# Eight-layer hybrid stack on one Trainium2 core: the index work of the last FFN half in blocks, a two-slot attention lag, and picks dealt by VectorE's load per slot

## What is computed

```python
# FFN 0 (128 -> 512 -> 512 -> 512 -> 128)
h = silu(_tlin(x, w1_w, w1_s)) * _tlin(x, w2_w, w2_s)
h = gelu(_tlin(h, h1_w, h1_s))
h = gelu(_tlin(h, h2_w, h2_s))
return _tlin(h, w3_w, w3_s)
# top-k attention, in batches of 128 queries in the reference's small shape; here one sequence of 2048
I = einsum('bths,h->bts', relu(einsum('bthd,bsd->bths', q_i, k_i)), idx_w)   # 4 index heads
I = where(local, inf, I); I = where(causal, -inf, I)
_, idx = top_k(I, 96)                       # 64 local keys and the 32 best others
key_c, value, kr_sel = rows of the picked keys
scores = (q_c . key_c + q_r . rope(kr_sel, rank)) * scale
out = softmax(scores) . value, then @ W_out
```

## Time and profile before

| | us |
|---|---|
| median of 3 runs (1315.41 to 1323.14) | 1317.44 |
| span of the profiled execution, first to last instruction | 1068.8 |
| PE busy in it | 941.6 |
| DVE busy | 786.1 |
| ACT busy | 692.7 |
| POOL busy | 583.4 |
| mean granted TensorE clock, as a share of 2.4 GHz | 0.893 |

### The profile page before, as it was taken

One profiled execution on the slowest core, in us unless ns is written; L12 is line 12 of the kernel. 1 busy time (PEld: TensorE's weight loads), 2 busy tenths in 40 slices (PEclk: granted clock), 3 DMA queues, 4 the chain that ended last, 5 costly groups with the idle time before them and its releaser, 6 DMA issues. The chain is left out here.

```text
span 1068.8 us, 19776 instructions
## 1 busy us (share of the span) xinstructions
PE 941.6 (88%) x6850; PEld 690.5 (65%) x6850; DVE 786.1 (74%) x1468; ACT 692.7 (65%) x1920; POOL 583.4 (55%) x622
## 2 busy tenths in 40 slices
PE   8999999999999977787889988888988897897786
PEld 5888868676767336556656666666767676576544
DVE  4888875757466788987895898797698979733346
ACT  5767655555564476694695678786687776656454
POOL 0111044333333777777777667777777777776001
PEclk9999999999999678997795689897798978989899
DMA  7100001000000563533522423331331333131001
GB/s 237 40 21 2 2 1 45 1 1 1 1 1 12 124 146 92 132 81 80 130 59 61 101 61 73 73 70 41 73 73 38 73 73 74 47 105 40 1 1 39
DMA packets 58737, 62.07 MB, mean 58 GB/s; under 512 B 27760, under 2 KB 43152, under 8 KB 58256
## 3 DMA queue, kind: packets, MB, share of 16 engines
q1 hardware_dynamic: 42768, 36.41, 13.2%
q0 software_dynamic: 15872, 24.41, 10.1%
HBM read 52.65 MB, written 8.13 MB: 57 GB/s over the span
## 5 line engine op out<-in xcount | busy, mean ns | idle before, releaser
L791 POOL DMA_INDIRECT gathered_rows<-key_table,idx_T x496 | 482.5, 973 | 157.6 <-issue 146.6
L2382 DVE TENSOR_TENSOR turned_rows<-bank,rank_rope 96x512 f32<-96x512 f32 x128 | 87.3, 682 | 83.3 <-PE bank L1293 82.1
L1293 PE MATMUL bank<-ident,gathered_rows 128*96 128x128 f32 x512 | 92.6, 311 | 11.8 <-DVE turned_rows L2382 7.1
L2356 DVE SCALAR_TENSOR_TENSOR index_sums<-index_relu,iw,index_sums 128x512 f32<-128x512 f32 (+4 forms) x114 | 75.4, 661 | 33.4 <-ACT index_relu L1826 30.8
L832 PE MATMUL bank<-index_k_hi,index_q 128*128 128x512 f32 (+5 forms) x160 | 77.2, 485 | 19.3 <-DVE idx_T L2376 11.6
L1826 ACT ACTIVATE index_relu<-bank 128x512 f32<-128x512 f32 (+4 forms) x152 | 75.1, 507 | 24.0 <-PE bank L832 23.6
L1848 ACT ACTIVATE probs<-masked_scores,attn_columns 128x208 f32<-128x208 f32 x128 | 59.5, 465 | 31.3 <-DVE attn_columns L2392 26.7
L832 PE MATMUL bank<-probs_window,local_values 80*32 80x128 f32 x256 | 57.4, 311 | 24.7 <-ACT probs_picked L1864 23.1
L1293 PEld LDWEIGHTS bank<-ident,gathered_rows 128*96 128x96 f32 x512 | 66.0, 144 | 20.5 <-issue 11.4
L2364 DVE MAX8 top<-index_sums 128x8 f32<-128x320 f32 (+13 forms) x56 | 75.8, 1354 | 1.0
L2366 DVE FIND_INDEX8 idx_u<-top,index_sums 128x8 uint32<-128x320 f32 (+13 forms) x56 | 75.5, 1348 | 0.0
(11 more groups left out here) (295 smaller groups left out, 2430.4 us busy)
## 6 DMA issues: line engine op xcount, KB each, us to landing
queries_in<-q_rot SPq DMA_DIRECT2D x32, 256.0 KB
gathered_rows<-key_table,idx_T POOLq DMA_INDIRECT x496, 2.5
q_rot<-rotated SPq DMA_DIRECT2D x16, 256.0 KB, 3.3
queries_in<-q_lat SPq DMA_DIRECT2D x16, 256.0 KB
h<-in_h SPq DMA_DIRECT2D x2, 1024.0 KB, 7.9
q_lat<-q_latent_sb SPq DMA_DIRECT2D x8, 256.0 KB
local_values<-key_table SPq DMA_DIRECT2D x15, 80.0 KB
rope_tables<-in_cos_ql SPq DMA_DIRECT2D x4, 256.0 KB
```

The costliest lines, as they stand in the source:

```text
L791: pool.indirect_dma_start(out=G[i % 2][:, gather_place(i, q), :], out_offset=None, in_=key_table[0:index_width(i), :], in_offset=bass.Indi ...
L1293: last = pe.transpose(bank[2][0:ROW, j * P:(j + 1) * P], G[i % 2][:, gather_place(i, 4 * g + j), :], ident[:])
L2356: v.scalar_tensor_tensor(s_, r_, iw[:, h:h + 1], s_, ALU.mult, ALU.add).then_inc(i_used, 1)
L2382: v.tensor_tensor(GT[n % 2].rearrange("r (j p) -> r j p", j=4), bank[2][0:ROW, :].rearrange("r (j p) -> r j p", j=4), rank_rope[:].unsquee ...
```

## The change

1. POOL no longer rounds the second gelus of R = 3. ACT takes the gelu twice, once into `a_hi` and once into `ffn_full` (`SELF_ROUNDED = 8`); DVE's subtraction waits for ACT. POOL goes from step 7 straight to `gather(0)`; `EARLY_GATHER` is gone.
2. `early_setup` moves everything ahead and into blocks: `raw` and `ik` after q = 0, `iq0` and `iq1` after 1, `iq2` and `iq3` after 2, the sums of tile 0 after 4 with `rows`, `cq` after 5. DVE does the whole pick of tile 0 after its q = 5 and that of tile 1 after its q = 9, with nothing between. PE turns tile 0 after q = 8 and tile 1 after q = 12, and projects `qp0` and `qp1` after 13 and 14, ahead of the downs.
3. The norm of chunks 2 and 3 leaves `topk_front` and is done in the loop (`loop_norm`, slots 7 to 9 and 26 to 28).
4. `ATTN_LAG` goes from 4 to 2, all `TAIL_SLOT` entries down by 2, and the regrouping of the first queries from slots 2 and 3 to slots 0 and 1. SP stores the first rotated queries ahead of the latents.
5. Picks are dealt by room: `other_work(s)` adds up DVE's other elements in a slot, and a slot gets `max(even - other_work(s), even / 4)`.

```diff
-        ATTN_LAG = 4
+        ATTN_LAG = 2
-        TAIL_SLOT = {0: 52, 1: 75, 2: 103, 3: 122}
+        TAIL_SLOT = {0: 50, 1: 73, 2: 101, 3: 120}
+        NORM_SLOT = {2: 7, 3: 26}
+        even = (all_picks + sum(other_work(s) for s in PICKED)) / len(PICKED)
+        room = [max(even - other_work(s), even / 4) for s in PICKED]
...
-                SLOT_STEPS[int(first + (last - first) * run / total) + (step[1] == "rows")].append(step)
+                SLOT_STEPS[slot_with_room(first + (last - first) * run / total) + (step[1] == "rows")].append(step)
...
-                for q in range(4 * NM):
+                for q in range(4 * NM if R < 3 else SELF_ROUNDED):
...
+                    if R == 3 and q >= SELF_ROUNDED:
+                        fn(a_hi[:, q % 8, :], bank[m], ACT.Gelu, scale=sc[:, m:m + 1])
                     fn(f_full[:, q % 4, :], bank[m], ACT.Gelu, scale=sc[:, m:m + 1]).then_inc(f_gelu, 1)
...
-            PICKS_AT = {6: (0, 0, 8), 7: (0, 8, 12), 8: (0, 12, 16), 11: (1, 0, 6), 12: (1, 6, 9), 13: (1, 9, 12), 14: (1, 12, 16)}
+            ENDS_AT = {0: ("ik",), 1: ("iq0", "iq1"), 2: ("iq2", "iq3")}
...
+            def loop_norm(c, k):
+                n = 4 * L_TOPK + c
+                if k == 0:
+                    pe.wait_ge(x_ready, n + 1)
+                    pe.wait_ge(ln_applied, LN0 + n)
+                    bank_released(c - 1, NPIECE - 2)
+                    mm(bank[3], center[:], chunk(x, c)).then_inc(ln_centered, 1)
+                elif k == 1:
+                    pe.wait_ge(ln_squared, n + 1)
+                    bank_released(c - 1, NPIECE - 1)
+                    mm(bank[5], ones[:], chunk(xn, c)).then_inc(ln_var, 1)
```

More of the change, by code:

```diff
@@ L529, in cost, with tail_cost, other_work, slot_with_room @@
             return sum(c for _, c in todo)
+        def tail_cost(g, k):
+            (name, n), W = TAIL[g][k], GROUP_TILES[g][1] * P
+            return {"var": W + 60, "unit": 2 * (HALF + 60), "down": W + 60, "kv": C + 2 * P + 180,
+                    "KV": 2 * P + 60, "lq": C + 60}.get(name, 0)
+        def other_work(s):
+            ends = [PIECES[k] for c, k in piece_ends_at(s)]
+            return (sum(C + 60 for name in ends if name[:2] in ("ik", "iq", "ra", "qp"))
+                    + sum(C + 60 for name in ends if name == "qp0") + 3 * (C + 60) * len(turns_at(s))
+                    + sum(tail_cost(g, k) for g, k in tail_at(s - 1)))
+        PICKED = range(1, PICK_SLOTS)
+        all_picks = cost(sum(SUMS[FRONT + 1:] + PICKS[FRONT:], []))
+        even = (all_picks + sum(other_work(s) for s in PICKED)) / len(PICKED)
+        room = [max(even - other_work(s), even / 4) for s in PICKED]
+        room_before = [sum(room[:k]) * all_picks / sum(room) for k in range(len(room) + 1)]
+        def slot_with_room(work):
+            k = max(k for k in range(len(room)) if room_before[k] <= work + 1e-6)
+            return PICKED[k]
         def spread(todo, first, last):
@@ L1178, in piece @@
                         bank_released(0, PIECES.index(released))
+                elif c == 0 and name[:2] == "qp":
+                    bank_released(0, PIECES.index("rows" if name == "qp0" else "cq"))
                 elif c == 0:
@@ L1215, in early_setup @@
             def early_setup(q):
-                if q == 1:
+                if q == 0:
                     pe.wait_ge(s_tk, N_TK)
                     piece(0, PIECES.index("raw"))
-                elif q == 2:
                     piece(0, PIECES.index("ik"))
-                    piece(0, PIECES.index("iq0"))
-                elif q in (3, 4, 5):
-                    piece(0, PIECES.index(f"iq{q - 2}"))
-                elif q == 6:
+                elif q in (1, 2):
+                    for h in (2 * q - 2, 2 * q - 1):
+                        piece(0, PIECES.index(f"iq{h}"))
+                elif q == 4:
+                    sums(0)
@@ L1226, in early_setup @@
                     piece(0, PIECES.index("rows"))
-                    sums(0)
+                elif q == 5:
+                    piece(0, PIECES.index("cq"))
                 elif q == 7:
-                    piece(0, PIECES.index("cq"))
-                elif q == 9:
                     sums(1)
-                elif q == 10:
+                elif q == 8:
                     index_turn(0)
+                elif q == 12:
+                    index_turn(1)
+                elif q in (13, 14):
+                    piece(0, EARLY + q - 13)
@@ L1249, in topk_front @@
-                norm_var(L_TOPK, 1)
-                for k in range(3, SETUP_FRONT):
-                    piece(1, k)
-                pe.wait_ge(ln_sd, norm_index(L_TOPK, 1) + 2)
+            def loop_norm(c, k):
[9 more added lines that the diff above has]
+                    mm(bank[5], ones[:], chunk(xn, c)).then_inc(ln_var, 1)
@@ L1663, in norm_square, with loop_norm @@
                     fn(chunk(xn, 2 * r + u), bank[4 + u], ACT.Square).then_inc(ln_squared, 1)
+            def loop_norm(c, k):
+                n, own = 4 * L_TOPK + c, chunk(xn, c)
+                if k == 0:
+                    act.wait_ge(ln_centered, n + 1)
+                    fn(own, bank[3], ACT.Square).then_inc(ln_squared, 1)
+                elif k == 1:
+                    act.wait_ge(ln_var, n + 1)
+                    steps.did(fn(own, bank[5], ACT.Ln, scale=1.0 / P, bias=eps_col))
+                    fn(own, own, ACT.Exp, scale=-0.5).then_inc(ln_sd, 1)
             def norm_spread(k, r, which=(0, 1)):
-                if (k, r) != (L_TOPK, 1) and which != (0,):
+                if which != (0,):
                     act.preload_act_table_set("natural_log_exp_and_others")
@@ L2307, in _ @@
             EARLY_PICKS = (SUMS[0] + PICKS[0][:-2], SUMS[1] + PICKS[1][:-2])
-            PICKS_AT = {6: (0, 0, 8), 7: (0, 8, 12), 8: (0, 12, 16), 11: (1, 0, 6), 12: (1, 6, 9), 13: (1, 9, 12), 14: (1, 12, 16)}
+            ENDS_AT = {0: ("ik",), 1: ("iq0", "iq1"), 2: ("iq2", "iq3")}
             def early_setup(q):
-                if 1 <= q < 6:
-                    piece_end(0, q - 1)
-                if q in PICKS_AT:
-                    i, first, last = PICKS_AT[q]
+                for name in ENDS_AT.get(q, ()):
+                    piece_end(0, PIECES.index(name))
+                if q in (5, 9):
+                    i = q // 4 - 1
                     assert len(EARLY_PICKS[i]) == 16
-                    for step, _ in EARLY_PICKS[i][first:last]:
+                    for step, _ in EARLY_PICKS[i]:
                         pick(*step)
-                    if last == 16:
-                        pick(i, "turn", 0)
-                if q == 10:
+                    pick(i, "turn", 0)
+                elif q == 7:
                     pick(0, "rows", 0)
+                elif q == 12:
+                    pick(1, "rows", 0)
             def topk_front():
-                pick(1, "rows", 0)
                 for k in (EARLY, EARLY + 1):
```

85 lines of the change are left out of this document (42 added, 43 removed).

## The result

| | median us | runs |
|---|---|---|
| before | 1316.43 | 1310.60 to 1323.14 |
| after | 1331.59 | 1327.76 to 1332.37 |

The ratio is 1.0142, with a 95% interval of 1.0108 to 1.0175: the change makes the kernel **slower by 1.4%**, where 1307.9 us, a gain, was forecast. 1331.59 lies above the range of 1300 to 1324 as well. First the page of the changed kernel: its span, busy us by engine, then tenths in 40 slices.

A forecast was written before the change was run, and what follows sets the result against it. POOL's gathers were taken to bound the kernel, just ahead of the slot loop. Gathers ending 3.4 + 6.1 = 9.5 us earlier cut the span from 1068.8 to 1059.3 us; with 248.6 us around it, 1307.9 us, range 1300 to 1324.

The forecast's parts named there:

- with the 248.6 us around it: Last step of the sum: time outside the program's span, added to the forecast span of 1059.3 us to give 1307.9 us.
- Part 1, the start of the gathers: POOL waits for tile 0's indices alone; first gather near 337.3 us, fifth near 342.9, 8.5 us earlier.
- Part 2, the turn of tile 1: PE idles about 4 us, a low clock follows, tile 1's gathers start 5 us late; POOL keeps 3.4 us.
- that rival: Clock holds or returns at once after PE's idle at tile 1's turn; POOL keeps 14.6 us, time 1302.8 us; chance 0.18.
- Part 3, the front: Ahead of the slot loop: DVE's slot 0 near 383 us against 376.88, 6 us later; at full clock 1 us earlier.
- Part 4, lag and dealing: In the slot loop: lag of two and dealing by room remove POOL's 6.1 us of stalls; group 127 at 979 us.
- So gathers end 3.4 + 6.1 = 9.5 us earlier: End of POOL's gathers: 3.4 us kept from the earlier start plus 6.1 us of removed stalls.
- The likeliest case: The forecast itself: gathers just decide the loop's end, time 1307.9 us, own range 1304 to 1311; chance 0.42.
- POOL is full: POOL in the gather stretch: 492 gathers at 0.97 + 0.30 us make 635 us, with only 6 us of real stalls.
- the loop rival: The slot loop, not the gathers, sets the end and evenness gives nothing: 1310 to 1317 us, middle 1313; chance 0.28.
- the slower one: Low clock stays in early slots and returns with denser picks of slots 100 to 111: 1324 us; chance 0.12.
- The tail is unchanged: After the gathers: some 81 us of work follow, which the change leaves alone.

The follow-up runs named there:

- the new trace of before: The kernel before, unchanged, profiled again: 1316.24 us, with spans of 1305.1 to 1322.4 us.
- the second trace of the changed kernel: The changed kernel, unchanged, run and profiled again beside the kernel before: 1330.77 us, ratio 1.0119, profiled span 1326.6 us.

## Why the prediction was wrong

**The step that failed first is the smallest in the working: "with the 248.6 us around it".** The span of before and its timed runs were 19% apart, and I named the difference instead of asking for it. Only 1.9 us lie around the program; of the rest, by the new trace of before, 32 us lie ahead of group 0 and 212 in the loop. The Trainium skill (Perfetto Trace Analysis, Summary: the profiler window per engine type) speaks of some 6.2 us between a profile's total and the reported time. That total isn't quite the span used here, but by either figure 248.6 us could not lie there. All terms that rest on the loop's rows were thus worked out for a regime that no timed run was in.

**Part 1, the start of the gathers: right.** First gather 337.66 (forecast 337.3), fifth 342.84 (342.9).

**Part 2, the turn of tile 1: right in the wait, half right behind it.** PE idled 3.37 us (4), and the 17th gather stood back 3.90 us and started at 361.45 (about 363). The low clock did not hold as in the earlier trace rows: the stretch from 354 to 371 was granted 0.82, not 0.51, so that rival was nearer. In the new trace of before PE idles the same 1.88 us ahead of its second down, and the stretch behind was granted 0.99: what the working took for the consequence of an idle of 1.88 us did not come back.

**Part 3, the front: right in the time, wrong as a term of the sum.** The sums of slot 0 start at 384.10 (383). But the working counted this as 6 us lost against 376.88. In the new trace of before they start at 393.17, and group 0 is rotated at 419.8 against 397.6: where the signals are held, the front gained 9 us at the sums and 22 at group 0. That the forecast time was met is in part luck.

**Part 4, lag and dealing: the step "So gathers end 3.4 + 6.1 = 9.5 us earlier" failed.** Stalls of 6.1 us are no limit where POOL waits 260 us for others (389.5 less 129.6). The last gather started at 1201.2 us, 14.6 us later than in the new trace of before (1186.6), not 9.5 us earlier: POOL was not full. The two slots fewer, a gain by the count of slots, put the attention closer to the index work, so that POOL waits and then gathers 32 times in one piece, and the loop stands still. Lag and dealing, which were to give 6.1 us, cost 33.

**The likeliest case's premise, "POOL is full",** was true of the one execution and of no timed one. Nor was any rival right: the loop rival expected 1310 to 1317 us and the slower one 1324 by a low clock. The slower rival had the place, the denser slots from 100 on (from group 88 to 108 the changed kernel took 161.2 us, before 137.6), but not the mechanism: with the gathers paced the long stops are gone at nearly the same granted clock (0.81 against 0.80), so it was the long runs of gathers.

**"The tail is unchanged": right.** From the rotation of group 127 to the end it is 81.6 us, in the new trace of before 81.5.

**Where the front's gain went,** by the second trace of the changed kernel against the new one of before: at group 16 it is 16.0 us ahead (502.1 against 518.1), at 88 15.4, at 104 4.0; at 108 it is 8.2 behind, at 127 11.5.

## What to carry to other kernels

Before a trace is read at all, hold its span against the timed runs. Here 1.9 us were the rule, and 248.6 us meant that the trace showed another regime, in which sums from its rows did not hold. Where gathers by index run beside a loop whose engines signal each other, don't let them run ahead as far as the buffers allow: let each group of them wait for the loop. In the kernel before that gave 45 us at a distance of 7 groups and 44 at 5. Which signal they wait for matters too: 1304.2 us by the turn, 1267.1 by the values. And a shorter lag is no gain in itself: it takes slack from the work that feeds the next stage, and that stage may give it back in one piece.

## What the runs showed of the hardware

- While gathers by index are under way, PE's signals are held: half of those on record in the loop were over 0.3 us late (344 of 662 in before, 321 of 650 in the changed kernel), up to 34.7 us, the stop of the changed kernel shown first. Of VectorE's and ScalarE's none on record is late, but a third are not on record. The last held signal mostly comes 1 to 2 us behind the last gather's end, behind the runs of 20 and more gathers 3.6 to 6.4 us (4.8 in that stop); that remainder isn't explained. Plain loads of the same size, from SP's or GpSimd's queue, hold none (latest 0.06 us).
- The Trainium skill (SBUF — State Buffer, SBUF: two separate sides) says that within the engines only the port pair of VectorE and GpSimd contends. No run here tests it or bears against it: at 708 us PE's matmuls start and follow each other as usual, only what tells others of their end is late. The profile's end of a matmul says nothing about its signal; the start of the one who waits does.
- The price is not in proportion: with two gathers a slot the time is 24 us over that with plain loads, with four 206 us when they are paced and 252 us when they aren't.
- Open: one profiled execution of the kernel before made the same gathers at the same pitch without a single held signal, and 250 us faster. What made the difference isn't known; no run here has repeated it. It is also the only trace with gathers by index in which the semaphores' moves are nearly all on record, so the recording itself is not ruled out as part of the cause.
